# Routing in two parts: three expert slots chosen from the first ten batches

## What is computed

```python
x = x + _L0_xattn_ref(_layernorm(x), ctx_1024, ctx_1024, Wq, bq, Wk, bk, Wv, bv, Wo, bo)
x = x + _L0_ffn_ref(_layernorm(x), wr, br, w1, b1, w2, b2)

def _L0_ffn_ref(x, wr, br, w1, b1, w2, b2):
    scores = einsum('bsh,he->bse', x, wr) + br
    expert_id = argmax(scores, axis=-1)
    h = gelu(einsum('bsh,ehf->ebsf', x, w1) + b1[:, None, None, :], approximate=False)
    y = einsum('ebsf,efh->ebsh', h, w2) + b2[:, None, None, :]
    return einsum('ebsh,bse->bsh', y, one_hot(expert_id, E))
```

## Time and profile before

| | us |
|---|---|
| median of 3 runs (372.34 to 374.41) | 373.86 |
| the profiled execution | 370.5 |
| its span, first to last instruction | 368.5 |
| TensorE busy, of the span | 330.0 (90%) |
| mean granted TensorE clock | 0.947 |

### The profile page before, as it was taken

The page is one execution under the profiler, slowest core; times in us unless marked ns, Lnnn a source line. Parts: engine busy times, 40 slices in busy tenths (PEclk is TensorE's granted clock), DMA queues, the critical chain, the costliest instruction groups (busy, mean ns, idle before and its releaser), DMA issues. The chain is left out here.

```text
span 368.5 us, 9161 instructions
## 1 busy us (share of the span) xinstructions
PE 330.0 (90%) x3303; PEld 283.8 (77%) x3303; DVE 155.7 (42%) x349; ACT 136.6 (37%) x427; POOL 153.1 (42%) x382
## 2 busy tenths in 40 slices
PE   6899999999999999753429999999999999999991
PEld 5677777777777777542119999999999999999991
DVE  2568777777777777743911111211121111112110
ACT  3555555555555555300005223322332332233220
POOL 5786666666666644331560223222322332231111
PEclk9999999999999999985558999999999999999997
DMA  6991554444200000000094564465456546764300
GB/s 175 319 323 45 158 170 145 145 146 149 90 30 31 30 30 31 30 30 29 9 355 149 192 228 167 170 239 192 177 187 229 195 161 195 216 206 137 120 0 0
DMA packets 28698, 51.87 MB, mean 141 GB/s; under 512 B 3117, under 2 KB 18607, under 8 KB 28528
## 3 DMA queue, kind: packets, MB, share of 16 engines
q1 hardware_dynamic: 24720, 43.00, 33.3%
q0 software_dynamic: 2944, 8.13, 8.2%
q10 hardware_dynamic: 992, 0.17, 0.3%
...
## 5 line engine op out<-in xcount | busy, mean ns | idle before, releaser
L470 ACT ACTIVATE hT<-bank,b_sb 128x128 f32<-128x128 f32 x184 | 52.7, 369 | 104.7 <-PE bank L904 104.5
L904 PEld LDWEIGHTS bank<-xeT,w_slot 128*128 128x128 f32 x736 | 87.2, 195 | 1.1
L904 PE MATMUL bank<-xeT,w_slot 128*128 128x128 f32 x736 | 87.3, 278 | 0.0
L918 PE MATMUL bank<-w_sb,hT 128*128 x368 | 83.1, 379 | 0.0
L338 POOL DMA_INDIRECT out<-y_sb,scatter_i x23 | 23.2, 1007 | 125.4 <-DVE y_sb L677 120.2
L918 PEld LDWEIGHTS bank<-w_sb,hT 128*128 128x128 f32 x368 | 68.2, 190 | 8.4
L662 DVE COPY xeT<-bank 128x256 f32<-128x256 f32 x23 | 9.8, 425 | 81.0 <-PE bank L894 81.0
L388 ACT ACTIVATE k_pair<-bank,bk_pair,own 128x128 f32<-128x128 f32 x64 | 24.1, 456 | 48.2 <-PE bank L744 48.2
L524 DVE TENSOR_REDUCE peaks<-bank 128x4 f32<-128x512 f32 x64 | 39.8, 685 | 0.9 <-PE bank L703 0.7
L409 ACT ACTIVATE probsT<-bank 128x512 f32<-128x512 f32 x64 | 33.0, 602 | 14.7 <-PE bank L780 14.7
L677 DVE TENSOR_TENSOR y_sb<-gathered,bank 128x256 f32<-128x256 f32 x23 | 9.7, 421 | 56.5 <-PE bank L918 56.5
...
## 6 DMA issues: line engine op xcount, KB each, us to landing
w_slot<-in_w SPq DMA_DIRECT2D x23, 1024.0 KB, 5.3
w_sb<-in_w SPq DMA_DIRECT2D x8, 1024.0 KB, 5.8
...
b_sb<-in_b SPq DMA_DIRECT2D x1, 1024.0 KB, 11.0
gathered<-records,gather_i POOLq DMA_INDIRECT x23, 3.8
out<-y_sb,scatter_i POOLq DMA_INDIRECT x23, 2.4
```

The costliest lines, as they stand in the source:

```text
L470: ins = a.activation(hT[:, s % 2, c], H_BANK[s % 2][c // 4][:, P * (c % 4):P * (c % 4 + 1)], ACT.Gelu, bias=b1_sb[:, bass.ds(e * FC + c, 1)])
L904: ins = t.matmul(H_BANK[s % 2][f // 4][:, P * (f % 4):P * (f % 4 + 1)], w1_slot[:, s % 2, c, P * f:P * (f + 1)], xeT[:, s % 2, c], start=( ...
L918: ins = t.matmul(Y_BANK[s % 2][:, 0:D], hT[:, s % 2, c], w2_flat[:, bass.ds(e * (FC * D) + c * D, D)], start=(c == 0), stop=(c == FC - 1))
```

## The change

The batches are split into a first stage (batches 0 to 9) and a second (10 to 15). Ten batches are 1280 tokens, which fill at least three whole slots whatever the routing. The first stage names three full slots while the last two batches are still in attention; they are gathered and go through the expert products while the remaining batches are routed. The second stage names the other 20 slots. The number of slots stays 23, and so do the products.

The ids are found in another way: `choose_tokens` compares every token's code (expert and tile of its rank) with every slot's code and multiplies by the token's number; one product per batch with `place_hot` gives the ids (`name_tokens`). `code_tok`, `code_hot` and `ids_T` are gone, and `place_hot` is made by one VectorE instruction per stage and some rows on GpSimd. `keep_used` works out how many tiles of each expert the first stage has used. GpSimd issues the first two gathers ahead of the normalisation of batch 14 and the third ahead of that of batch 15. SyncE loads the `w1` of slots 0 and 1 ahead of the saves of batches 13 to 15. ScalarE's gelu is called by halves, so that the last batch's copies can stand between them. The router's product of batch 15 goes to another PSUM bank, because the banks of `up(1)` are in use by then.

```diff
+    FIRST = 10
+    EARLY = 3
+    LATE = SLOTS - EARLY
...
-        DVE_ROWS = 10
+        STAGES = ((0, FIRST, 6), (FIRST, NB, 13))
...
+                sp.wait_ge(sm["slots_done"], 1)
+                load_up_weights(0)
+                load_up_weights(1)
+                for b in range(FIRST + 3, NB):
+                    save_record(b)
+                load_up_weights(2)
+                sp.wait_ge(sm["slots_done"], 2)
+                for s in range(EARLY, SLOTS):
+                    load_up_weights(s)
...
+                g.memset(onehot[:], 0.0)
+                g.memset(used[:], 0.0)
+                g.memset(one_col[:], 1.0)
...
+            def place_rows(stage):
+                lo, hi, mid = STAGES[stage]
+                pool.wait_ge(sm["places_done"], stage + 1)
+                for b in range(mid, hi):
+                    g.tensor_scalar(place_hot[:, b], iota_row[:], place[:, b:b + 1], one_col[:], ALU.is_equal, ALU.mult)\
+                        .then_inc(sm["place_hot_pool"], 1)
...
+                add_bo(b)
+                if b == NB - 2:
+                    place_rows(0)
             pool.wait_ge(sm["index_done"], 1)
...
+            wait_records(FIRST)
+            pool.wait_ge(sm["x1_done"], 2 * EARLY)
+            gather(0)
+            gather(1)
+            normalize_x1(NB - 2)
+            gather(2)
+            normalize_x1(NB - 1)
+            place_rows(1)
+            pool.wait_ge(sm["index_done"], 3)
+            wait_records(NB)
+            for s in range(EARLY, EARLY + AHEAD):
                 gather(s)
...
+                a.reg_load(reg, slot_e_i[0:1, 0:1])
+                gelu(0, 0, reg)
+                gelu(0, 1, reg)
+                take_x2T(NB - 1)
+                a.reg_load(reg, slot_e_i[0:1, 1:2])
+                gelu(1, 0, reg)
+                take_logits(NB - 1)
+                gelu(1, 1, reg)
+                a.reg_load(reg, slot_e_i[0:1, 2:3])
+                gelu(2, 0, reg)
+                gelu(2, 1, reg)
+                act.wait_ge(sm["slots_done"], 2)
...
+            def choose(stage):
...
+                link(v.tensor_tensor(logits[:, lo:hi], logits[:, lo:hi], br_sb[:].unsqueeze(1).broadcast_to(by_expert), ALU.add))
...
+                v.tensor_tensor(onehot[:, lo:hi], keyed[:, lo:hi], key[:, lo:hi].unsqueeze(2).broadcast_to(by_expert),
+                                ALU.is_equal).then_inc(sm["onehot_done"], 1)
+                dve.wait_ge(sm["onehot_done"], stage + 1)
+                link(v.tensor_scalar(e_code[:, lo:hi], key[:, lo:hi], -float(TILES), float(E * TILES), ALU.mult, ALU.add))
...
+            def find_places(stage, bank):
...
+                dve.wait_ge(sm["rank_ready"], stage + 1)
+                link(v.tensor_scalar(n_i[:], bank[:, m * E:(m + 1) * E], float((P - 1) * stage), None, ALU.add))
+                v.tensor_tensor(ranked[:, lo:hi], bank[:, 0:m * E].rearrange("p (b e) -> p b e", e=E), onehot[:, lo:hi],
+                                ALU.mult).then_inc(sm["rank_taken"], 1)
+                dve.wait_ge(sm["rank_taken"], stage + 1)
+                link(v.tensor_reduce(rank[:, lo:hi], ranked[:, lo:hi], AX_X, ALU.add))
+                link(v.tensor_copy(rank_i[:, lo:hi], rank[:, lo:hi]))
+                link(v.tensor_scalar(place_i[:, lo:hi], rank_i[:, lo:hi], P - 1, None, ALU.bitwise_and))
+                v.tensor_copy(place[:, lo:hi], place_i[:, lo:hi]).then_inc(sm["places_done"], 1)
+                link(v.tensor_scalar(tile_i[:, lo:hi], rank_i[:, lo:hi], 7, None, ALU.logical_shift_right))
+                link(v.tensor_tensor(code[:, lo:hi], tile_i[:, lo:hi], e_code[:, lo:hi], ALU.add))
...
+            def place_rows(stage):
+                lo, hi, mid = STAGES[stage]
+                dve.wait_ge(sm["places_done"], stage + 1)
+                by_place = [P, mid - lo, P]
+                v.tensor_tensor(place_hot[:, lo:mid], iota_row[:].unsqueeze(1).broadcast_to(by_place),
+                                place[:, lo:mid].unsqueeze(2).broadcast_to(by_place), ALU.is_equal)\
+                    .then_inc(sm["place_hot_dve"], 1)
+
+            def count_tiles(stage):
+                link(v.tensor_scalar(n_sh[:], n_i[:], 7, None, ALU.logical_shift_right))
...
+                link(v.tensor_tensor(ends[:, 0, PAD:], tiles[:], used[:, 0:E], ALU.subtract))
...
+                    link(v.tensor_tensor(ends[:, k + 1, PAD:], ends[:, k, PAD:], ends[:, k, PAD - shift:PAD + E - shift], ALU.add))
+
+            def name_slots(stage):
...
+                link(v.tensor_tensor(past, index.unsqueeze(2).broadcast_to(by_slot),
+                                     ends[:, 3, PAD:].unsqueeze(1).broadcast_to(by_slot), ALU.is_ge))
+                v.tensor_reduce(slot_e[:, first:last], past, AX_X, ALU.add)
...
+                link(v.tensor_reduce(slot_sum[:, first:last], past_gap, AX_X, ALU.add))
+                v.tensor_scalar(slot_e_i[:, first:last], slot_e[:, first:last], float(E - 1), None, ALU.min)\
+                    .then_inc(sm["slots_done"], 1)
+                link(v.tensor_tensor(slot_code[:, first:last], slot_sum[:, first:last], base, ALU.add))
...
+            def keep_used():
+                link(v.tensor_tensor(used[:, 0:E], ends[:, 3, PAD:], tiles[:], ALU.subtract))
+                link(v.tensor_scalar(used[:, 0:E], used[:, 0:E], -1.0, float(EARLY), ALU.mult, ALU.add))
+                link(v.scalar_tensor_tensor(out=used[:, 0:E], in0=used[:, 0:E], scalar=0.0, in1=tiles[:], op0=ALU.max, op1=ALU.min))
+                link(v.tensor_scalar(used_16[:], used[:, 1:E + 1], float(TILES), None, ALU.add))
+                link(v.tensor_scalar(late_f[:], slot_f[:, EARLY:SLOTS], -float(EARLY), None, ALU.add))
+                link(v.tensor_scalar(late_used[:], late_f[:], used[:, 0:1], None, ALU.add))
+
+            def choose_tokens(stage):
...
+                if stage > 0:
+                    dve.wait_ge(sm["ids_ready"], stage)
+                link(v.tensor_tensor(hit[:, 0:hi, 0:last - first], code[:, 0:hi].unsqueeze(2).broadcast_to(by_slot),
+                                     slot_code[:, first:last].unsqueeze(1).broadcast_to(by_slot), ALU.is_equal))
+                v.tensor_tensor(chosen[:, 0:hi, 0:last - first], hit[:, 0:hi, 0:last - first],
+                                tok1[:, 0:hi].unsqueeze(2).broadcast_to(by_slot), ALU.mult).then_inc(sm["chosen_done"], 1)
+
+            def take_ids(stage, bank):
+                first, last = ((0, EARLY), (EARLY, SLOTS))[stage]
+                dve.wait_ge(sm["ids_ready"], stage + 1)
...
+                dve.wait_ge(sm["ids_taken"], stage + 1)
+                v.tensor_scalar(gather_i[:, first:last], ids[:, first:last], -1.0, 0.0, ALU.add, ALU.max)\
+                    .then_inc(sm["index_done"], 1)
...
+            for b in range(NB):
+                maxima(b)
...
+                if b == NB - 2:
+                    find_places(0, V_BANK)
+                if b == NB - 1:
+                    place_rows(0)
+                shift_queries(b)
...
+                if b == NB - 1:
+                    choose_tokens(0)
...
+                if b == NB - 3:
+                    choose(0)
+                if b == NB - 2:
+                    count_tiles(0)
+                if b == NB - 1:
+                    take_ids(0, V_BANK)
                 if live(b - 1):
...
-            v.tensor_scalar(gather_i[:], ids[:], -1.0, 0.0, ALU.add, ALU.max).then_inc(sm["index_done"], 1)
-            link(v.tensor_scalar(ids_pad[:], ids[:], 0.0, float(OUT_OF_BOUNDS), ALU.is_equal, ALU.mult))
-            v.scalar_tensor_tensor(out=scatter_i[:], in0=ids[:], scalar=-1.0, in1=ids_pad[:],
-                                   op0=ALU.add, op1=ALU.add).then_inc(sm["index_done"], 1)
+                if b == NB - 2:
+                    name_slots(0)
...
                 take_xe(0)
                 take_xe(1)
                 add_b2(0)
...
+                add_b2(1)
+                take_xe(2)
+                choose(1)
+                find_places(1, M_BANK)
+                place_rows(1)
+                count_tiles(1)
+                name_slots(1)
+                choose_tokens(1)
+                finish(0)
+                take_ids(1, M_BANK)
+                add_b2(2)
+                finish(1)
+                dve.wait_ge(sm["slots_done"], 2)
+                take_xe(3)
+                add_b2(3)
+                finish(2)
+                take_xe(4)
+                for s in range(EARLY, SLOTS):
...
+            def count_ranks(stage, bank):
...
+                pe.wait_ge(sm["onehot_done"], stage + 1)
+                t.matmul(bank[:, 0:(m + 1) * E], before[:], onehot[:, lo:hi + 1].rearrange("p b e -> p (b e)"), start=True, stop=False)
+                for b in range(hi):
+                    later = max(b + 1 - lo, 0)
+                    ins = t.matmul(bank[:, later * E:(m + 1) * E], ones[:],
```

(44 more changed lines are left out.)

311 lines of the change are left out of this document (135 added, 176 removed).

## The result

The changed kernel takes 359.86 us (median of four runs), the kernel before 373.1 us beside it, also of four. That ratio is 13.4 us less (11.3 to 15.4). The profiled run took 356.86 us with a span of 355.1 us, against 368.5 before: 13.4 less in the span too. The forecast was 17.3 less, 356.5 us, with a range of 352.5 to 363.5.

The account below looks back on a forecast made before the run. The experts were taken as bound by TensorE alone, after a gap waiting for normalisation and routing. Starting `up(0)` 23.2 us earlier, plus 5.85 of added work and waits, gave -17.3: 373.86 to 356.5 us, range 352.5 to 363.5.

Parts of the forecast that it names:

- late start: Rival, chance 0.05: first gather goes out only behind the last normalisation, `up(0)` starts at 178.0; change -9.1, 364.8 us.
- up(0) at 169.75: First expert product on TensorE starts at 169.75 us instead of 192.91, 23.2 us earlier.
- `keep_used` 1.25 on the path: Six small VectorE instructions ahead of `take_xe(0)` add 1.25 us to the path to `up(0)`.
- Cold start at `up(0)` cancels, 1.4: Slow-clock products at the start of `up(0)` cost 1.4 us before and the same now, so no change.
- Wait at `name_tokens(1)` 2.7: TensorE stands 2.7 us in the middle of `up(2)`, waiting for VectorE's second-stage routing chain.
- the rival of a longer chain: Rival, chance 0.20: second-stage routing links cost 0.33 us each, TensorE waits 2.4 more; change -14.9, 358.9 us.
- Between `up(0)` and `up(3)` 29.0: TensorE's stretch from the first slot's `up` to slot 3's, including second-stage routing work and waits, with `up(3)` near 199 us.
- The rival of a second cold start: Rival, chance 0.10: the 2.7 us wait lets TensorE's clock fall, products after pay 1.4 again; change -15.9, 357.9 us.
- the wait of 0.15: TensorE waits 0.15 us after the first half of `down(0)` for `choose(1)` in the second routing chain.
- No wait from `up(3)` on: From slot 3's `up` to the end TensorE never waits, at 7.245 us a slot.
- The rule weighed: GpSimd sharing SBUF interfaces with VectorE could double its three second-stage rows to 5.5 us, making the change -16.6.
- at half throughout: Rival, chance 0.03: clock stays at half while expert and routing work alternate up to `up(3)`; +2.6 us, 376.5.

Follow-up runs that it names:

- again: The changed kernel run once more with no edit; 359.37 us, ratio 0.9631 to the kernel before.
- fillname: The changed kernel plus 12 unread identity transposes on TensorE ahead of `name_tokens(1)`; 356.03 us, ratio 0.9551 to the kernel before.
- combo: Changed kernel with `keep_used`, `name_tokens(1)` and part of `find_places(0)` later, seven `place_hot` rows on GpSimd, `turn_xe(4)` in the middle of `up(3)`; 354.55 us, ratio 0.9542.
- gatherslast: The changed kernel with the three early gathers issued behind the normalisations of batches 14 and 15; 364.12 us, ratio 0.9800 to the kernel before.
- fillafter: The changed kernel, order kept, plus 43 unread identity transposes in TensorE's waits from 152 us on; 352.84 us, ratio 0.9483 to the kernel before.
- fill: The combo kernel plus 29 unread identity transposes in TensorE's waits; 350.14 us, ratio 0.9387 to the kernel before.
- idsalone: The kernel before with only the new way to the ids and nothing early; 369.02 us, ratio 0.9933 to the kernel before.

## Why the prediction was right, and where it was off

The mechanism was right: three slots' work goes into the gap, the end follows `up(0)` one for one, and the time is in the forecast's range. The size was 4 us too large. The change of -13.4 lies outside my own -19 to -16, which had a chance of 0.54, and just past the -14 at which the unknown costs ended. What covers it is the room that I had added for scatter and for a late start, and the late start did not happen: that the range held is in part luck. By its own steps:

- **up(0) at 169.75**: it was 171.73, 2.0 us later. The trace of the kernel after is 0.6 us late from its start, since a load of a weight landed later. The casts beside GpSimd took 0.9 more than three times 0.17, part of it into idle time. The wide instruction took 1.20; I took 0.95 between bounds of 0.7 and 1.75. From the division of batch 14 to its residual another 0.8 was lost, since the clock fell already in the shifted scores, which took 1.74 us.
- **`keep_used` 1.25 on the path**: 1.22. But it also lengthened TensorE's wait ahead of `up(0)` to 2.27 us, behind which `up(0)` ran slow.
- **Cold start at `up(0)` cancels, 1.4**: 4.82 - 3.74 = 1.1 us in the profiled run, 2.6 in that of *again*. It cancels against before, but the product could have run at full clock.
- **Wait at `name_tokens(1)` 2.7**: 2.72. The second chain took 6.26 us (183.38 to 189.64) where its links had been priced at 6.05, 6.2 with the hand-over; the rival of a longer chain is out.
- **Between `up(0)` and `up(3)` 29.0**: 29.9. This is the step that failed: "clock 1.00 behind it". The rival of a second cold start, at 0.10 and 1.4 us, is what happened; *fillname* shows cause and price, 3.0 us by the medians' ratios. In the profiled run it cost 1.8; the sum is only 0.9 too small because four groups of small products took 1.6 us and not 2.35, the wait of 0.15 did not come, and the first cold start was 0.3 cheaper. I had argued from the loop's waits of up to 1.2 us that leave the clock full, but this wait was 2.7. The trace of before spoke against the argument too. There the projection of batch 14, the row under this paragraph, took 1.89 us where that of batch 15 took 1.13 (162.27), and from 155 to 157 us the clock was 0.55. The waits ahead of it were 0.72 and 0.97 us. The Trainium skill (TensorE: Matmul & The Clock Gate, HAM oscillation) describes kernels that are throttled again at each wait; the trace of the kernel after agrees, with three falls.

```profile
154.97 1.89 PE L808 MATMUL bank<-wo_sb,oT 128*128 128x256 f32 x4
```

- **No wait from `up(3)` on**: 145.8 against 144.8 us from there to the last product. `turn_xe(4)` is issued behind `up(3)`, and its copy stands bare before `up(4)`; *combo* removes it.
- **The rule weighed**: I had applied the sharing of interfaces to GpSimd's rows. Those took 0.79 us each (2.38 for three), no longer than the 0.91 of before. The price was on the other side, in VectorE's small conversions.
- **The other rivals**: the early part did not start late (the first gather at 159.47 us; *gatherslast* priced that at 6.3 us, not 8.2), and the clock was not at half throughout.

Together: 2.0 + 0.9 + 1.0 = 3.9 us, which is the 17.3 forecast less the 13.4 measured.

What stays open: which wait tips the clock. That it is the waits is shown by the kernels that fill them. Nine of the profiled runs have the early slots and no transposes in this stretch. In five of them TensorE had waited 1.39 us or more just ahead of the projection of batch 15, which took 1.19 to 1.79; in the other four it had waited 0.98 or less, and the projection took 1.13. But the length of one wait does not decide it: 1.75 us left the clock full in *fillafter* and not in *fill*. And in *idsalone* the projection of batch 14 took 1.13 us, behind the same waits of 0.72 and 0.97 us behind which it took 1.89 in the kernel before.
